# One MoE layer's dispatch inside an attention loop: TensorE's unrolled program becomes a loop of two turns, and GpSimd writes the rows that are sent out

## The chip, the cores and the metric

One NeuronCore of one Trainium2 chip. The metric is the device time of one execution in microseconds: the kernel before takes 3282.54 us, the median of 3 runs (3276.01 to 3284.56).

## What is computed

Four layers on 128 x 64 tokens of width 128 (8192 rows). Each layer adds a cross-attention with 16 heads and then a feed-forward network (FFN), both scaled by the tanh of a gate:

```python
x = x + tanh(g_xattn[l]) * xattn_l(layernorm(x), ctx, ctx)
x = x + tanh(g_ffn[l])   * ffn_l(layernorm(x))
```

Keys and values come from ctx, 64 per sequence. The FFN of layer 0 is a mixture of 8 experts with the best two taken, that of layer 1 takes the best one, that of layer 2 is a single fp8 product, and that of layer 3, whose first part the change touches, is again a mixture with two of eight experts:

```python
probs = softmax(x_flat @ router_w.T)
top_k_probs, top_k_idx = top_k(probs, 2)
cw = weights of the two, normalised by their sum
output = sum over e of cw[:, e] * (new_gelu(x_flat @ w1[e].T + b1[e]) @ w2[e].T + b2[e])
```

## The kernel before

The 8192 rows of x stay in SBUF as 64 tiles of 128 tokens. A chunk is four tiles (512 tokens), and there are CHUNKS = 16. Each attention goes through the chunks in turns: in turn u TensorE (PE) works on the attention of chunk u in four slots s = 0 to 3, one tile a slot: `scores` (L1096, psS), `p_turn` (L1105, the transposes of the softmax numerators into psT), `weigh` (L1119, weights times V into psO, and L1125, the row sums into psY). Between them lie the projections of the next chunks (`q_proj`, `k_proj`, `v_proj`), the turning of the normalised x (L1045, into psX) and the output projection of the chunk before (L1146, psX). VectorE (DVE) takes the maximum (L1541) and subtracts it (L1543), ScalarE (ACT) takes the exponential (L750) and copies the turned numerators (L756); at the end of a turn ACT inverts the row sums (L761, L763 into rden), and DVE scales the output once (L1548, one instruction per turn). GpSimd (POOL) does small steps of the layernorm (L470, L472) and adds the bias to x (L510, `x_bias`); SyncE loads ctx and spreads K into a block-diagonal kexp with 16 DMAs per turn. Attentions 0 to 2 run as loops of two turns (`Fori`) on every engine.

The last attention (layer 3) is written out on all engines (`attention_routed`), because the first half of the mixture, the dispatch, is computed inside it, some turns behind the attention:

- DVE, in turn u, takes the statistics of chunk u - 2 (`stats`, L1650 and L1653) in slot 1 and writes its normalised rows (`apply`, L1663, four TENSOR_SCALARs of 128x128) in slot 3 into a **ring** of four group buffers. A group is two chunks (8 tiles); a row has 132 elements: 128 of the token and four with its number and gates. Two buffers of the ring are in gio, one in w_ffn, one in gio3.
- PE turns the rows of chunk u - 3 from the ring (`turn_x`, L1195), multiplies by the router's weights (`route`, L1201), and in every odd turn from 5 on ranks a group's tokens within their experts by products with triangular and all-one matrices (`rank`, L1207 to L1211, into psX). The last of these products adds the counts of all groups before, kept in macc, which has two halves used in turn.
- ACT copies the logits and the ranks out of PSUM (L835 for the ranks). After a rank PE waits for that copy (semaphore rk) before it uses psX again, for L1045.
- DVE takes the routing decision of a group in 32 small steps (L1641), each of which counts up one semaphore, m_seq; steps 18 and 19 (`counts`) update macc.
- POOL does the small steps of the mixture's norm (`norm`, L560 and L562), then `x_bias`, then the **scatters**: every group is sent to the DRAM buffer xg by 16 indirect DMAs (L569) of 128 rows each, eight for the first choice in even turns from 6 on (`scatter(g, 0)`, which waits for the group's last step on DVE), eight for the second in odd turns from 7 on (`scatter(g, 1)`, without a wait). A group buffer may be rewritten when its 16 scatters have landed (semaphore sd); DVE's `apply` waits for that at the first chunk of a group from the fifth group on.

Turns run to 20 on POOL; from turn 16 on no attention is left. L1305 and L1904 stand in another stage, the first dispatch (layer 0), which also scatters rows: L1305 are products of the shared expert, L1904 reads them.

Of the kernel before, what the change touches and what calls it, by code (L numbers as in the profile page):

```python
# [61 lines left out]
def program(nc, a, out):  # L62
# [4 lines left out]
    with ExitStack() as ctx:  # L67
# [72 lines left out]
        ring.append(gio3[:, :, :])  # L140
        lgt = sb("lgt", [P, GT * E])
# [294 lines left out]
        def _(pool):  # L436
# [116 lines left out]
            def attention_routed(lay):  # L553
# [473 lines left out]
        def _(pe):  # L1027
# [159 lines left out]
            def attention_routed(lay):  # L1187
# [3 lines left out]
                def turn_x(c):  # L1191
                    e.wait_ge(m["xn"], c + 1)
                    e.wait_ge(x_up, K0 + lay * CHUNKS + c + 2 if c + 2 <= CHUNKS else K0 + (lay + 1) * CHUNKS)
# [4 lines left out]
                def route(c):  # L1198
                    e.wait_ge(m["xt_sb"], c + 1)
# [4 lines left out]
                def rank(g):  # L1204
                    e.wait_ge(m["seq"], MSTEPS[lay] * g + 18)
# [5 lines left out]
                    e.matmul(out8, ones16[:, :], macc[:, lay // 3, g % 2, :].rearrange("p (a x) -> p a x", a=1)  # L1211
# [13 lines left out]
                for u in range(CHUNKS + 4):  # L1225
                    inside = u < CHUNKS
                    c = u - 3
                    for s in range(LT):
                        if inside:
                            scores(lay, None, *ahead(u, s, 2))  # L1230
                        if s == 1 and inside:
                            q_proj(lay, None, u + 1)
                        if s == 1 and 0 <= c < CHUNKS:
                            turn_x(c)
                        if s == 2 and 0 <= c < CHUNKS:
                            route(c)
                        if s == 3 and 0 <= c < CHUNKS:
                            e.wait_ge(m["lg"], c + 1)
                        if s == 3 and u >= 5 and u % 2 == 1:
                            rank((u - 5) // 2)  # L1240
                        if inside:
                            p_turn(lay, None, *ahead(u, s, 1))
                        if s == 3 and u >= 5 and u % 2 == 1:
                            e.wait_ge(m["rk"], (u - 5) // 2 + 1)
                        if s == 3 and u + 2 <= CHUNKS:
                            ln_t(ATT[lay], None, u + 2)
                        if inside:
                            weigh(lay, None, u, s)
                        if s == 0 and inside:
                            v_proj(lay, None, u + 1)  # L1250
                        if s == 2 and inside:
                            k_proj(lay, None, u + 2)
                        if s == 3 and 0 < u <= CHUNKS:
                            out_proj(lay, None, u - 1)
                e.wait_ge(m["seq"], MSTEPS[lay] * (NG - 1) + 20)
                e.matmul(psO[:, 0:E], ones16[:, :], macc[:, lay // 3, NG % 2, :], start=True, stop=True).then_inc(m["cnt_ps"], 1)
# [12 lines left out]
            def dispatch(lay):  # L1269
# [64 lines left out]
                e.matmul(psO[:, 0:E], ones16[:, :], macc[:, lay // 3, NG % 2, :], start=True, stop=True).then_inc(m["cnt_ps"], 1)  # L1334
# [141 lines left out]
        def _(dve):  # L1476
# [143 lines left out]
            def attention_routed(lay):  # L1620
# [615 lines left out]
```

## Time and profile before

| | before |
|---|---|
| median of 3 runs | 3282.54 us (3276.01 to 3284.56) |
| the profiled execution | 3298.21 us |
| its span | 3296.4 us |
| mean granted clock of TensorE | 0.886 |
| PE, matmul / weight load | 2532.8 us (77%) / 1794.6 us (54%) |
| DVE / ACT | 1566.6 us (48%) / 1380.2 us (42%) |
| POOL | 978.3 us (30%) |
| the last attention, first to last L1548 | 2424.0 to 2828.3 us |

The rows further down are of this one profiled execution, 15.7 us above the median; its times count from the start of the span. PE stands for TensorE's matmuls and PEld for its weight loads, which run beside them. A share of the span is an average over stages of very different kinds: the attentions take turns of PE, DVE and ACT, the second halves of the mixtures are limited in other ways. "Idle before" is the time an engine stood still ahead of an instruction, with what released it; "issue" means that it waited for nothing the profile shows, and "remote" that it waited for a semaphore whose sender the profile does not name.

### The profile page before, as it was taken

What the parts mean: (1) busy time and instruction counts of PE and PEld (TensorE: products, weight loads), DVE (VectorE), ACT (ScalarE), POOL (GpSimd) and SP (SyncE); (2) the same over time, 40 slices, a digit from 0 to 9 for tenths busy, and PEclk for the clock granted to TensorE, in tenths of its full rate; (3) what the DMA queues carried; (4) which work ended last, traced back from release to release, by engine and by line L of the source; (5) the groups of instructions that cost most, each with busy time, mean ns of one, the idle gap of its engine ahead of it and who ended that gap; (6) DMA issues with size and microseconds to landing.
All of it is one profiled execution on the core that took longest, in us unless ns stands there. A gap on an engine that the chain in (4) does not pass through costs nothing. (4 is left out here: it accounts for less than half of the span.)

```text
span 3296.4 us, 74894 instructions
## 1 busy us (share of the span) xinstructions
PE 2532.8 (77%) x28202; PEld 1794.6 (54%) x28202; DVE 1566.6 (48%) x4283; ACT 1380.2 (42%) x1992; POOL 978.3 (30%) x1052
## 2 busy tenths in 40 slices
PE   4888864439997799989999969993288777358883
PEld 2555543328886455567777735551145444247773
DVE  3555544424443577622222247776667665513322
ACT  2555533213332466644545436661055444124441
POOL 4444426634444112110000000001112433634444
PEclk9999976669999899989999979996599888679997
DMA  3010101126665222100000011110011111146666
GB/s 98 22 24 20 23 16 38 39 80 195 197 192 153 78 53 61 34 3 0 0 0 0 1 44 45 41 41 11 11 32 31 37 35 37 44 144 191 189 186 219
DMA packets 143775, 219.56 MB, mean 67 GB/s; under 512 B 27177, under 2 KB 94513, under 8 KB 143026
## 3 DMA queue, kind: packets, MB, share of 16 engines
q1 hardware_dynamic: 96930, 90.25, 10.8%
q10 hardware_dynamic: 29232, 90.37, 8.8%
q0 software_dynamic: 17408, 36.21, 3.2%
q8 instruction: 128, 2.10, 0.3%
q14 instruction: 77, 0.63, 0.1%
HBM read 157.48 MB, written 43.61 MB: 61 GB/s over the span
## 5 line engine op out<-in xcount | busy, mean ns | idle before, releaser
L1541 DVE TENSOR_REDUCE mx<-psS 128x16 f32<-128x1024 f32 x264 | 322.6, 1222 | 321.9 <-PE psS L1096 294.1
L650 POOL DMA_INDIRECT yg<-ysb,yidx x288 | 279.5, 970 | 421.0 <-DVE ysb L2005 190.6
L470 POOL TENSOR_TENSOR ve<-mv,eps 128x4 f32<-128x4 f32 x102 | 20.3, 199 | 1184.4 <-DVE mv L1517 1182.3
L756 ACT ACTIVATE work<-psT 128x1024 f32<-128x1024 f32 x260 | 266.2, 1024 | 215.5 <-PE psT L1105 214.8
L750 ACT ACTIVATE work<-work 128x1024 f32<-128x1024 f32 x264 | 278.3, 1054 | 135.9 <-DVE work L1543 132.7
L1096 PE MATMUL psS<-kexp,qT 64*64 64x512 f32 x2112 | 307.6, 634 | 31.0 <-DMA kexp<-kT 15.3
L1543 DVE TENSOR_TENSOR work<-psS,mx 128x1024 f32<-128x1024 f32 x264 | 323.2, 1224 | 9.1
L1105 PEld LDWEIGHTS psT<-ident,work 128*128 128x128 f32 x2080 | 239.6, 145 | 151.5 <-issue 99.8
L1105 PE MATMUL psT<-ident,work 128*128 128x128 f32 x2080 | 288.3, 283 | 5.3 <-ACT work L756 3.3
L1381 PEld LDWEIGHTS psY<-w_ffn,work 128*128 128x128 f32 x2016 | 247.8, 192 | 9.4 <-DVE work L1976 1.2
L1381 PE MATMUL psY<-w_ffn,work 128*128 128x128 f32 x2016 | 248.5, 275 | 1.6 <-DVE ysb L1999 1.0
L1045 PE MATMUL psX<-ident,xn 128*128 128x128 f32 x408 | 78.9, 326 | 133.1 <-DVE xn L1528 103.2
L1119 PE MATMUL psO<-work,v 128*32 128x64 f32 x8192 | 172.6, 226 | 7.1 <-issue 4.4
L1125 PE MATMUL psY<-work,ones 128*32 128x128 f32 x4096 | 170.4, 279 | 5.5 <-issue 5.0
L1431 PEld LDWEIGHTS psO<-w_ffn,work 128*128 128x128 f32 x1024 | 131.3, 192 | 60.0 <-issue 49.7
L1431 PEld LDWEIGHTS psY<-w_ffn,work 128*128 128x128 f32 x1024 | 131.9, 192 | 53.5 <-issue 53.5
L1119 PEld LDWEIGHTS psO<-work,v 128*32 128x32 f32 x8192 | 130.6, 112 | 53.9 <-issue 43.4
L614 POOL DMA_INDIRECT xg<-gio,posi x128 | 125.3, 979 | 103.7 <-DVE gio L1867 64.3
L1045 PEld LDWEIGHTS psX<-ident,xn 128*128 128x128 f32 x408 | 53.5, 164 | 180.8 <-DVE xn L1528 82.3
L1528 DVE TENSOR_SCALAR xn<-x_sb,mv,rstd 128x128 f32 (+1 forms) x408 | 117.6, 352 | 66.5 <-POOL rstd L472 60.9
L1548 DVE TENSOR_TENSOR aT<-psO,rden 128x512 f32<-128x512 f32 x64 | 44.2, 691 | 196.0 <-ACT rden L763 177.2
L1431 PE MATMUL psO<-w_ffn,work 128*128 128x128 f32 x1024 | 133.2, 276 | 3.0 <-ACT work L889 2.9
(278 smaller groups left out, 4645.0 us busy)
## 6 DMA issues: line engine op xcount, KB each, us to landing
w_ffn<-in_wmoe ACTq DMA_DIRECT2D x72, 578.0 KB
w_ffn<-in_wmoe ACTq DMA_DIRECT2D x72, 576.0 KB
ctxT<-in_ctxT SPq DMA_DIRECT2D x76, 256.0 KB, 2.8
xin<-xg SPq DMA_DIRECT2D x144, 132.0 KB
kexp<-kT SPq DMA_DIRECT2D x1152, 16.0 KB
gio<-yg SPq DMA_DIRECT2D x16, 512.0 KB, 3.9
work<-yg SPq DMA_DIRECT2D x16, 512.0 KB, 6.4
yg<-ysb,yidx POOLq DMA_INDIRECT x288
```

Source lines behind the costliest of these rows:

```text
L650: e.indirect_dma_start(out=yg, out_offset=bass.IndirectOffsetOnAxis(ap=yidx[:, b, t:t + 1], axis=0), in_=ysb[:, b, t, :], in_offset=None, ...
L750: e.activation(sc[:, s % 2], sc[:, s % 2], ACT.Exp).then_inc(p_ok, 1)
L756: e.activation(pT[:, s % 2, :], psT[:, :], ACT.Copy).then_inc(pt_ok, 1)
L1045: m = e.transpose(psX[:, t * P:(t + 1) * P], xn[:, t, :], ident[:, :])
L1096: m = e.matmul(psS[64 * half:64 * half + 64, 512 * k:512 * k + 512], qT[64 * k:64 * k + 64, b, c:c + SEQ], kexp[64 * k:64 * k + 64, b, :, ...
L1105: m = e.transpose(psT[:, r * P:(r + 1) * P], sc[:, s % 2, 2 * r:2 * r + 2, :].rearrange("p a b -> p (a b)"), ident[:, :])
L1119: e.matmul(psO[32 * c:32 * c + 32, s * P + 64 * half:s * P + 64 * half + 64], v2[:, b, 2 * s + half, 64 * c + 16 * hi:64 * c + 16 * hi + 3 ...
L1125: m = e.matmul(psY[32 * c:32 * c + 32, s * P:(s + 1) * P], ones2[:, hi, :], pT[:, s % 2, at:at + P], start=(hi == 0), stop=(hi == 1))
L1381: mm = e.matmul(psY[:, t * D:(t + 1) * D], mh[:, b, k * SLOT + t * P:k * SLOT + (t + 1) * P], w[:, d0 + k * D:d0 + (k + 1) * D], start=(k ...
L1431: m = e.matmul(y[:, t * D:(t + 1) * D], hbuf[:, n % 4, t * P:(t + 1) * P], w_ffn[:, 2048 + hb * D:2048 + (hb + 1) * D], start=(hb == 0 and ...
L1541: e.tensor_reduce(mx[:, :], src, AX, ALU.max).then_inc(s_max, 1)
L1543: e.tensor_tensor(sc[:, s % 2], src, over_keys(mx[:, :]), ALU.subtract).then_inc(s_sub, 1)
```

## The change

Three things change, all in the last attention:

- PE's turns 4 to 13 become a loop of five passes of two turns (`e.Fori(0, (CHUNKS - 6) // 2)`). Turns 0 to 3 and 14 to 19 stay written out. The waits inside the loop compare with a register that the loop counts up.
- The rows that PE turns come from a new buffer of one chunk, xnf, which has the same address in every turn. DVE's `apply` writes there; it waits until the chunk before has been turned (xt_ps) and no longer for the scatters. macc has one half in use instead of two, so that its address too is the same in every turn; DVE waits for the rank product before it updates it.
- The ring is filled by GpSimd: `rows(c)` computes the same normalised rows again from x, behind `x_bias` and ahead of the scatters. It waits for the scatters that last used the buffer, and counts up the semaphore nrm, for which `scatter(g, 0)` and DVE's `stats` (with the number of two chunks before) now wait.

```diff
+        xnf = sb("xnf", [P, LT, D])
...
+                def rows(c):
+                    b = (c % 2) * LT
+                    if c >= 8 and c % 2 == 0:
+                        e.wait_ge(m[f"sd{c // 2 % 4}"], 16 * 2 * GT * (c // 8))
+                    e.wait_ge(m["rstd"], c + 1)
+                    for t in range(LT):
+                        mm = e.tensor_scalar(ring[c // 2 % 4][:, b + t, 0:D], xs(None, c, t), mmv[:, b + t, 0:1],
+                                             mrstd[:, 1, b + t:b + t + 1], ALU.subtract, ALU.mult)
+                    mm.then_inc(m["nrm"], 1)
+
                 def scatter(g, c):
                     if c == 0:
                         e.wait_ge(m["seq"], MSTEPS[lay] * (g + 1))
+                        e.wait_ge(m["nrm"], 2 * g + 2)
...
                     if u < CHUNKS:
                         x_bias(lay, None, u)
+                    if 2 <= u < CHUNKS + 2:
+                        rows(u - 2)
                     if u >= 6 and u % 2 == 0:
                         scatter((u - 6) // 2, 0)
...
-                        mm = e.transpose(psX[:, t * P:(t + 1) * P], ring[c // 2 % 4][:, c % 2 * LT + t, 0:D], ident[:, :])
+                        mm = e.transpose(psX[:, t * P:(t + 1) * P], xnf[:, t, :], ident[:, :])
...
-                    e.matmul(out8, ones16[:, :], macc[:, lay // 3, g % 2, :].rearrange("p (a x) -> p a x", a=1)
+                    e.matmul(out8, ones16[:, :], macc[:, lay // 3, 0, :].rearrange("p (a x) -> p a x", a=1)
...
-                for u in range(CHUNKS + 4):
+
+                def turn(i, u):
                     inside = u < CHUNKS
...
+                for u in range(4):
+                    turn(None, u)
+                with e.Fori(0, (CHUNKS - 6) // 2) as i:
+                    turn(i, 4)
+                    turn(i, 5)
+                for u in range(CHUNKS - 2, CHUNKS + 4):
+                    turn(None, u)
...
                 def stats(c):
...
                         e.wait_ge(m["xn"], c - 1)
+                        e.wait_ge(m["nrm"], c - 1)
...
                 def apply(c):
                     b = c % 2 * LT
-                    if c >= 8 and c % 2 == 0:
-                        e.wait_ge(m[f"sd{c // 2 % 4}"], 16 * 2 * GT * (c // 8))
+                    if c >= 1:
+                        e.wait_ge(m["xt_ps"], c)
...
-                        mm = e.tensor_scalar(ring[c // 2 % 4][:, b + t, 0:D], xs(None, c, t), mmv[:, b + t, 0:1],
+                        mm = e.tensor_scalar(xnf[:, t, :], xs(None, c, t), mmv[:, b + t, 0:1],
...
                     step(e.tensor_reduce, mcol[:, 8, :], mask16[:, :, :].rearrange("p t x -> p x t"), AX, ALU.add)
-                    step(e.tensor_tensor, macc[:, lay // 3, (g + 1) % 2, :], macc[:, lay // 3, g % 2, :], mcol[:, 8, :], ALU.add)
+                    e.wait_ge(m["rank_ps"], g + 1)
+                    step(e.tensor_tensor, macc[:, lay // 3, 0, :], macc[:, lay // 3, 0, :], mcol[:, 8, :], ALU.add)
```

The instructions of PE where its loop now begins, slots 0 and 1 of turn 4 (the line, the operation, out<-in, the shape, and how many in a row). Before:

```order
L1096 MATMUL psS<-kexp,qT 64x512 x4
L1105 MATMUL psT<-ident,work 128x128 x8
L1119 MATMUL psO<-work,v 32x64 x16
L1125 MATMUL psY<-work,ones 32x128 x8
L1064 MATMUL psQ<-w_att,ctxT 64x64 x16
L1096 MATMUL psS<-kexp,qT 64x512 x4
L1071 MATMUL psQ<-xT,w_att 128x512
L1195 MATMUL psX<-ident,gio 128x128 x4
L1105 MATMUL psT<-ident,work 128x128 x8
```

and now, with a branch into the loop and register instructions ahead of the groups whose addresses or waits the loop counts:

```order
L1277 UNCONDITIONAL_BRANCH
L1277 ISA
L1110 MATMUL psS<-kexp,qT 64x512 x4
L1115 REGISTER_ALU
L1119 MATMUL psT<-ident,work 128x128 x8
...
L1065 REGISTER_ALU
L1078 MATMUL psQ<-w_att,ctxT 64x64 x16
...
L1207 REGISTER_ALU
L1209 MATMUL psX<-ident,xnf 128x128 x4
```

The matmuls stand in the same order; the turning of the rows reads xnf instead of gio, and behind turn 5 a branch leads back to the start.

On POOL in the last attention, turn 7, an odd one, whose scatters have no wait of their own. Before:

```order
L470 TENSOR_TENSOR ve<-mv,eps 128x4
L472 TENSOR_TENSOR rstd<-ve,mhalf 128x4
L560 TENSOR_SCALAR mrstd<-mmv 128x4
L562 TENSOR_TENSOR mrstd<-mrstd,mhalf 128x4
L510 TENSOR_TENSOR x_sb<-x_sb,gbo 128x512
L569 DMA xg<-gio,posi 69632x132 x8
```

and now:

```order
L471 TENSOR_TENSOR ve<-mv,eps 128x4
L473 TENSOR_TENSOR rstd<-ve,mhalf 128x4
L561 TENSOR_SCALAR mrstd<-mmv 128x4
L563 TENSOR_TENSOR mrstd<-mrstd,mhalf 128x4
L511 TENSOR_TENSOR x_sb<-x_sb,gbo 128x512
L572 TENSOR_SCALAR w_ffn<-x_sb,mmv,mrstd 128x128 x4
L581 DMA xg<-gio,posi 69632x132 x8
```

Four instructions came in between x_bias and the eight scatters; nothing else moved on this engine.

## Rows read from the trace of the kernel before

**Rows 1.** The page's first part: engine busy us (share of the span) xinstructions.

```profile
PE 2532.8 (77%) x28202; PEld 1794.6 (54%) x28202; DVE 1566.6 (48%) x4283; ACT 1380.2 (42%) x1992; POOL 978.3 (30%) x1052
```

**Rows 2.** L1548 in attentions 1, 2, last; last from 2480 to 2525: first and last start.

```profile
L1548 DVE TENSOR_TENSOR aT<-psO,rden x14: 690/690/692, 1137.1 to 1381.7; 128x512 f32<-128x512 f32 x14
...
L1548 DVE TENSOR_TENSOR aT<-psO,rden x15: 690/692/693, 1975.9 to 2240.5; 128x512 f32<-128x512 f32 x15
...
L1548 DVE TENSOR_TENSOR aT<-psO,rden x16: 690/691/693, 2424.0 to 2828.3; 128x512 f32<-128x512 f32 x16
...
L1548 DVE TENSOR_TENSOR aT<-psO,rden x3: 691/691/693, 2482.0 to 2523.9; 128x512 f32<-128x512 f32 x3
```

**Rows 3.** Windows as long as two turns: attention 1, the last attention.

```profile
core 0: us, PE busy (x) PEld busy (x) DVE busy (x) ACT busy (x) POOL busy (x), PEclk, DMA share, GB/s
1249.30:1286.60 37.30, 35.35 (x643) 22.23 (x642) 27.91 (x46) 24.51 (x31) 7.44 (x8) 1.00 0.21 56
...
2644.30:2705.50 61.20, 46.09 (x642) 28.82 (x643) 36.77 (x100) 25.91 (x37) 23.39 (x26) 0.83 0.14 36
```

**Rows 4.** Waits in 2583 to 2644: us in total, times, longest us.

```profile
DVE aT L1548 <- ACT rden L763: 15.2, 2, 10.0
...
ACT rden L761 <- remote: 8.7, 1, 8.7
ACT rnk L835 <- remote: 7.9, 1, 7.9
```

**Rows 5.** Timeline, turn 6: start us, us, engine, line, instruction [idle before <-releaser].

```profile
2539.56 1.10 POOL L569 DMA_INDIRECT xg<-gio,posi  x1 [3.21 <-DVE gio L1641]
...
2542.41 0.17 PEld L1125 LDWEIGHTS psY<-work,ones 128*32 128x32 f32 x3 [0.58 <-issue]
...
2543.93 0.27 PE L1125 MATMUL psY<-work,ones 128*32 128x128 f32 x1 [0.39 <-issue]
...
2548.62 0.97 POOL L569 DMA_INDIRECT xg<-gio,posi  x1 [0.30 <-issue]
...
2551.90 0.60 ACT L761 ACTIVATE rden<-psY 128x512 f32<-128x512 f32 x1 [8.66 <-remote]
```

**Rows 6.** Timeline, turn 11, an odd one.

```profile
2690.18 1.10 POOL L569 DMA_INDIRECT xg<-w_ffn,posi  x1 [0.16 <-issue]
...
2694.00 0.19 PE L1211 MATMUL psX<-macc,ones 128*128 128x64 bf16 x1
...
2699.26 0.97 POOL L569 DMA_INDIRECT xg<-w_ffn,posi  x1 [0.30 <-issue]
...
2702.11 0.22 ACT L835 ACTIVATE rnk<-psX 128x64 f32<-128x64 f32 x1 [6.81 <-remote]
...
2702.38 1.12 PE L1045 MATMUL psX<-ident,xn 128*128 128x128 f32 x4 [7.29 <-ACT rnk L835]
```

**Rows 7.** DMA queues from 2536.5 to 2555: packets, MB, share of 16 engines.

```profile
q0 software_dynamic: 256, 0.54, 9.0%
q1 hardware_dynamic: 256, 0.26, 7.8%
```

**Rows 8.** DMA queues over six turns, 2583 to 2767: PE's instruction packets.

```profile
q8 instruction: 15, 0.25, 0.6%
```

**Rows 9.** Timeline of the first dispatch stage, within a burst of scatters.

```profile
588.87 2.05 PE L1305 MATMUL psY<-w_ffn,work 128*128 128x128 f32 x8 [5.50 <-DVE x_sb L1904]
...
595.59 0.75 DVE L1904 SCALAR_TENSOR_TENSOR x_sb<-psY,tg,x_sb 128x512 f32<-128x512 f32 x1 [6.87 <-issue]
```

**Rows 10.** DMA queues in the loop of attention 2, 2100 to 2200: all there are.

```profile
q1 hardware_dynamic: 3472, 3.97, 17.0%
```

**Rows 11.** Groups on POOL: busy us, mean ns of one, idle before.

```profile
L510 POOL TENSOR_TENSOR x_sb<-x_sb,gbo 128x512 f32<-128x512 f32 x6 | 7.7, 1286 | 0.0
...
L560 POOL TENSOR_SCALAR mrstd<-mmv 128x4 f32<-128x4 f32 x6 | 1.4, 238 | 0.0
```

**Rows 12.** Timeline of POOL, first scatter of turn 16.

```profile
2834.29 1.10 POOL L569 DMA_INDIRECT xg<-gio,posi  x1 [0.71 <-issue]
```

More of the change, by code:

```diff
@@ L1189, in attention_routed, with turn_x, route @@
                 m = MO[lay]
-                def turn_x(c):
-                    e.wait_ge(m["xn"], c + 1)
-                    e.wait_ge(x_up, K0 + lay * CHUNKS + c + 2 if c + 2 <= CHUNKS else K0 + (lay + 1) * CHUNKS)
+                def turn_x(i, u):
+                    e.wait_ge(m["xn"], val(i, u, 1, -2))
+                    e.wait_ge(x_up, val(i, min(u, CHUNKS + 1), 1, K0 + lay * CHUNKS - 1))
                     for t in range(LT):
-                        mm = e.transpose(psX[:, t * P:(t + 1) * P], ring[c // 2 % 4][:, c % 2 * LT + t, 0:D], ident[:, :])
+                        mm = e.transpose(psX[:, t * P:(t + 1) * P], xnf[:, t, :], ident[:, :])
                     mm.then_inc(m["xt_ps"], 1)
-                def route(c):
-                    e.wait_ge(m["xt_sb"], c + 1)
+                def route(i, u):
+                    e.wait_ge(m["xt_sb"], val(i, u, 1, -2))
                     for t in range(LT):
@@ L1202, in route, with group, rank @@
                     mm.then_inc(m["r_ps"], 1)
-                def rank(g):
-                    e.wait_ge(m["seq"], MSTEPS[lay] * g + 18)
+                def group(i, u, per, plus):
+                    return per * ((u - 5) // 2) + plus if i is None else i * per + (per * ((u - 5) // 2) + plus)
+                def rank(i, u):
+                    e.wait_ge(m["seq"], group(i, u, MSTEPS[lay], 18))
                     out8 = psX[:, GT * E:2 * GT * E].rearrange("p (t x) -> p t x", t=GT)
@@ L1224, in attention_routed @@
                 p_turn(lay, None, 0, 0)
-                for u in range(CHUNKS + 4):
+                def turn(i, u):
                     inside = u < CHUNKS
-                    c = u - 3
+                    routed = 3 <= u < CHUNKS + 3
+                    ranked = u >= 5 and u % 2 == 1
                     for s in range(LT):
                         if inside:
-                            scores(lay, None, *ahead(u, s, 2))
+                            scores(lay, i, *ahead(u, s, 2))
                         if s == 1 and inside:
[L1232 to L1240, printed above, removed]
+                            q_proj(lay, i, u + 1)
+                        if s == 1 and routed:
+                            turn_x(i, u)
+                        if s == 2 and routed:
+                            route(i, u)
+                        if s == 3 and routed:
+                            e.wait_ge(m["lg"], val(i, u, 1, -2))
+                        if s == 3 and ranked:
+                            rank(i, u)
@@ L1241, in attention_routed @@
                         if inside:
-                            p_turn(lay, None, *ahead(u, s, 1))
-                        if s == 3 and u >= 5 and u % 2 == 1:
-                            e.wait_ge(m["rk"], (u - 5) // 2 + 1)
+                            p_turn(lay, i, *ahead(u, s, 1))
+                        if s == 3 and ranked:
+                            e.wait_ge(m["rk"], group(i, u, 1, 1))
                         if s == 3 and u + 2 <= CHUNKS:
-                            ln_t(ATT[lay], None, u + 2)
+                            ln_t(ATT[lay], i, u + 2)
@@ L1247, in attention_routed @@
                         if inside:
-                            weigh(lay, None, u, s)
+                            weigh(lay, i, u, s)
                         if s == 0 and inside:
-                            v_proj(lay, None, u + 1)
+                            v_proj(lay, i, u + 1)
                         if s == 2 and inside:
-                            k_proj(lay, None, u + 2)
+                            k_proj(lay, i, u + 2)
                         if s == 3 and 0 < u <= CHUNKS:
-                            out_proj(lay, None, u - 1)
+                            out_proj(lay, i, u - 1)
@@ L1255, in attention_routed @@
+                for u in range(4):
[5 more added lines that the diff above has]
+                    turn(None, u)
                 e.wait_ge(m["seq"], MSTEPS[lay] * (NG - 1) + 20)
-                e.matmul(psO[:, 0:E], ones16[:, :], macc[:, lay // 3, NG % 2, :], start=True, stop=True).then_inc(m["cnt_ps"], 1)
+                e.matmul(psO[:, 0:E], ones16[:, :], macc[:, lay // 3, 0, :], start=True, stop=True).then_inc(m["cnt_ps"], 1)
@@ L1333, in dispatch @@
                 e.wait_ge(m["seq"], MSTEPS[lay] * NG)
-                e.matmul(psO[:, 0:E], ones16[:, :], macc[:, lay // 3, NG % 2, :], start=True, stop=True).then_inc(m["cnt_ps"], 1)
+                e.matmul(psO[:, 0:E], ones16[:, :], macc[:, lay // 3, 0, :], start=True, stop=True).then_inc(m["cnt_ps"], 1)
             def experts(lay):
```

## The prediction, before the run

> **What bounds the kernel now.** The page says TensorE (PE) is busy for 77% of the span [rows 1]; a share says nothing of one stage, so I went to the last attention and asked for the pace of its turns. L1548 runs once per turn on VectorE (DVE), so the distance between its first and last start, divided by the turns between, is the pace [rows 2]. In attention 1 it is (1381.7 - 1137.1) / 13 = 18.8 us, in attention 2 (2240.5 - 1975.9) / 14 = 18.9 us; PE runs a loop in both. In the last attention, where PE's program is written out, it is (2828.3 - 2424.0) / 15 = 27.0 us. Turns 4 and 5 of it, with routing but no scatters yet, take (2523.9 - 2482.0) / 2 = 20.9 us each (last row of the group). The busy time per stretch adds [rows 3]: two turns of attention 1 take 37.3 us, with PE busy for 35.4 of them and granted 1.00 of its clock; two turns with scatters take 61.2 us, with PE busy for 46.1 at a mean clock of 0.83. From turn 6 to turn 15, then, each turn loses about 30.6 - 20.9 = 9.7 us, some 97 us in all. The change aims at this stretch, and everything hangs on what causes the loss.
>
> The waits name it [rows 4]: ScalarE (ACT) waits 8.7 us before L761 and 7.9 us before L835, both times for semaphores of PE that the profile books as "remote". In an even turn [rows 5] the eight scatters of GpSimd (POOL) run from 2539.56 to 2549.6. From 2541.7 on PE's program, issued by whole groups before, comes a few instructions at a time with 0.6 to 1.2 us between (one such pause in the rows); the last L1125 is issued at 2543.93, and L761, which only needs that, starts at 2551.90, two microseconds after the last scatter. In an odd turn [rows 6] PE trickles nothing: the rank product L1211 is issued at 2694.00 and takes 0.19 us, but L835 sees it at 2702.11, again 1.9 us after the end of the burst (2699.26 + 0.97 = 2700.2), and PE then stands still for 7.3 us waiting for L835. So PE's signals come late as long as a burst runs.
>
> **Is it the fetching of instructions?** That is what a loop on PE would remove. Between 2536.5 and 2555.0, all 512 packets that the DMA engines move belong to the scatters and to the spread of K; none is an instruction packet [rows 7], and yet this stretch holds a full stall. Over three pairs of turns PE does fetch, 15 packets for 2 x 3 turns [rows 8], but the stall is as long without one as with one, and in the odd turn every instruction up to the wait was issued in time. The first dispatch stage, which scatters too and spreads no K, shows the same lateness: the product L1305 ends at 590.9, its reader L1904 starts at 595.59 [rows 9]. I therefore tie the loss to the burst of scatters, not to the way PE's program is stored. The bursts stay.
>
> **The change part by part.**
> - *PE's loop over turns 4 to 13.* It removes fetches that I price at nothing. A loop of this size needs none once it runs: in 100 us of attention 2 q1 alone carries packets [rows 10]. The costs are the register instructions (hidden: attention 1 with them keeps 18.65 us a turn) and the entry. 13 x 18.65 is 242.5 against the 244.6 that [rows 2] give, so the entry costs 2.1 us at most; 0 is the other bound, I take **+1.0**.
> - *What a rule says against it.* Every back edge could cost as much as the entry; [rows 2, 3] show it does not. The Trainium skill (Runtime: NRT & Kernel Launch, section Instruction fetch mechanics) says that a taken branch out of the buffered window forces a fetch and that kernels therefore prefer unrolled code. By that rule the four back edges would be paid each time; the trace does not agree, as attention 1 holds 18.65 us with a back edge every second turn.
> - *DVE's L1663 writes xnf instead of the ring.* Same four operations, same length: 0. Its wait on the scatters of four groups before goes (it is in no row of [rows 4], so nothing is won) and one on the previous turning of xnf comes, which lies two slots back in PE's order: 0. The new wait of L1650 on GpSimd's rows of two chunks before: 0 as long as POOL is not a turn behind. The new wait of macc on the rank product: behind it on DVE stands only L1548, which waits for ACT's L763, and so for PE's signals, up to 10.0 us anyway [rows 4]: 0.
> - *POOL's rows().* Four TENSOR_SCALARs of 128x128 per chunk, 16 chunks, behind x_bias and ahead of the scatters. The trace has no such row on POOL. Below: L560, 128x4, 0.24 us; above: L510, 128x512 of two inputs, 1.29 us [rows 11]. L510 less the fixed 0.24 is 2.05 ns a column; with one tensor read instead of two I halve that: 0.24 + 128 x 1.0 ns = 0.37 us, **1.5 us a chunk** (bounds 1.0 and 5.1). The Trainium skill (GPSIMD Engine Reference, section When to use GPSIMD) calls an elementwise operation of one input roughly line-rate and one of two inputs about twice as slow; halving the column part is in line with that, while at the two-input rate a chunk would cost 2.0 us and the sum 4 us more.
> - *Where those 1.5 us lie.* In an even turn the scatters wait for DVE's gates behind 3.2 us of idle POOL [rows 5]: hidden. In an odd turn the first scatter follows x_bias at once, with 0.16 us between [rows 6]: the burst starts 1.5 us later and, since PE's signals come back about 1.9 us after its end, so does the next turn. Turns 7, 9, 11, 13, 15: 5 x 1.5 = **+7.5**. Behind turn 15 only POOL's scatters are left, back to back until the barrier; rows() of chunks 14 and 15 stand ahead of them, less the 0.7 us that POOL idles there now [rows 12]: 3.0 - 0.7 = **+2.3**.
>
> Sum: 1.0 + 7.5 + 2.3 = +10.8 us. The profiled execution took 3298.21 us, 15.7 above the median of the runs (3282.54); on it the sum gives 3309.0, on the median 3293.3. About 0.3%, 9.8 us, is what a measurement of this kernel can tell from no change, so the forecast sits on that edge.
>
> **Rivals.**
> - *A, the loop cures the stall.* For: the trickle hits PE only where its program is written out, PE's idle time there is booked as issue, and no stage has both a loop on PE and scatters, so nothing refutes it directly. Against: [rows 6, 7, 9]. Turns 6 to 13 would run at 20.9 us: 4 pairs x (61.2 - 41.8) = -77.6. POOL has room: eight scatters 1.27 us apart, which [rows 6] span with 10.0 us, and some 5 us of small operations. Left of the costs: turn 15, tail, entry, 4.8. Net -72.8: **3209.7**, faster.
> - *A', only the even turns' trickle is fetching*, the odd turns' lateness is not: 4 x -9.7 = -38.8, and the costs of the forecast stay, 10.8: -28.0, **3254.5**.
> - *B, POOL is slow at these operations*, each like L510: 5.1 us a chunk. Odd turns 5 x 5.1 = 25.7, even turns 5 x (5.1 - 3.2) = 9.5, tail 9.5, entry 1: +45.7, **3328.2**. It decides from 3.2 us a chunk on, where even turns lose too.
> - *C, back edges cost like the entry*: 2.1 more for each of four and 1.1 at the entry, +9.5 on the forecast: **3302.8**.
>
> **How the numbers follow.** The forecast gets 0.56: three separate observations speak for it, but the cause of the late signals is not known. Its own range is 3284 to 3303 (below: the shifted burst costs the odd turns nothing and the entry is free, which leaves 2.3; above: 2.0 us a chunk and a full entry, 10.0 + 3.3 + 2.1 = 15.4; and some noise on both sides); half of it lies above +9.8. A gets 0.20, A' 0.14, B 0.06, C 0.04. Faster: A + A' = 0.34. Slower: half of the forecast, B and C = 0.38. Within 0.3%: 0.28. The range must reach down to A for 8 in 10, since the forecast with A' and C holds only 0.74: 3203 to 3306, with B left out.
>
> **What would show it.** If I am right, L835 and L761 still wait 7 to 9 us each for "remote", pairs of turns take 62 to 63 us, odd bursts start 1.5 us later behind x_bias, and the GpSimd row of 128x128 reads 0.3 to 0.5 us. Pairs of 42 to 45 us in the loop while turn 14 still stalls mean A; short even turns alone mean A'. A burst of scatters with no late signal would make the whole reading of the stall wrong.

## The result and the profile after

The changed kernel takes 3287.75 us, the median of 9 runs (3283.48 to 3295.73), beside 3277.81 us (3273.41 to 3285.88, 9 runs) of the kernel before on the same chip. The ratio is 1.0025, with a 95% interval of 1.0014 to 1.0036: 8 us slower by the ratio, within 0.3% (the two medians lie 9.9 us apart). The prediction said 3293.3 us, +10.8 on the kernel before. The sum came close, but two of its terms were wrong in opposite directions, and the stall under it was about three quarters smaller in every later run that scatters in the turns. Both are told below.

The profiled execution of the changed kernel took 3286.43 us, 1.3 below its median (that of before stood 20 above the median of its 9 runs). Against [rows 1], GpSimd (POOL) is busy 53 us longer and VectorE (DVE) 10 us; the page's first part:

```profile
PE 2537.8 (77%) x28202; PEld 1793.4 (55%) x28202; DVE 1576.8 (48%) x4283; ACT 1380.3 (42%) x1992; POOL 1031.0 (31%) x1116
```

The instruction that runs once per turn, now L1575, in the last attention (duration min/median/max, first and last start), answers to the third of [rows 2]:

```profile
L1575 DVE TENSOR_TENSOR aT<-psO,rden x16: 691/692/693, 2412.4 to 2817.6; 128x512 f32<-128x512 f32 x16
```

That is 405.2 us for 15 turns, and was 404.4 (404.36 and 405.20 with one more digit). Two turns in the window view, beside the last of [rows 3]:

```profile
core 0: us, PE busy (x) PEld busy (x) DVE busy (x) ACT busy (x) POOL busy (x), PEclk, DMA share, GB/s
2634.70:2696.30 61.60, 48.25 (x645) 29.03 (x641) 37.64 (x101) 25.82 (x36) 29.84 (x34) 0.83 0.13 35
```

61.6 us for two turns, and 61.2 before: the loop took nothing off. The stall is there in the loop too. The waits of two turns in the loop, 2572 to 2634 (us in total, times, longest):

```profile
POOL ve L471 <- DVE mv L1544: 26.9, 2, 13.7
DVE aT L1575 <- ACT rden L777: 19.4, 2, 10.4
ACT rden L775 <- remote: 16.5, 2, 9.1
```

Against [rows 4], the wait for the row sums now comes in both turns (L775, once L761), and the wait for the rank is no longer among those for "remote". An odd turn shows why (the rank product is now L1228, its reader L849):

```profile
2620.97 1.11 POOL L581 DMA_INDIRECT xg<-gio,posi  x1 [0.18 <-issue]
...
2621.86 0.19 PE L1228 MATMUL psX<-macc,ones 128*128 128x64 bf16 x1
...
2622.09 0.22 ACT L849 ACTIVATE rnk<-psX 128x64 f32<-128x64 f32 x1 [1.71 <-PE psX L1228]
```

The product comes 0.9 us into the burst, where it came 3.8 us into it before [rows 6], and is seen 0.04 us after its end. GpSimd's rows hold the burst back, and TensorE works on meanwhile. The timeline of one burst in the loop shows what [rows 5] showed for the written-out program:

```profile
2590.11 1.11 POOL L581 DMA_INDIRECT xg<-gio,posi  x1 [0.18 <-issue]
...
2592.37 0.15 PEld L1139 LDWEIGHTS psY<-work,ones 128*32 128x32 f32 x3 [0.61 <-issue]
...
2593.11 0.38 PE L1139 MATMUL psY<-work,ones 128*32 128x128 f32 x2 [0.32 <-issue]
...
2599.19 0.97 POOL L581 DMA_INDIRECT xg<-gio,posi  x1 [0.30 <-issue]
...
2602.34 0.60 ACT L775 ACTIVATE rden<-psY 128x512 f32<-128x512 f32 x1 [9.13 <-remote]
```

TensorE (PE) begins to trickle 2 us into the burst, its last row-sum product starts at about 2593.1, and ScalarE (ACT) sees it at 2602.34, 2.2 us after the burst's end (2599.19 + 0.97 = 2600.16). And there is nothing to fetch for PE: from 2510 to 2760 these are all the queues that carry packets, and the one that brings PE's instructions (q8, [rows 8]) is not among them:

```profile
q1 hardware_dynamic: 3392, 4.40, 7.7%
q0 software_dynamic: 2048, 4.33, 5.3%
q14 instruction: 7, 0.06, 0.1%
```

What GpSimd's rows cost stands in its groups (busy us, mean ns of one), 2572 to 2756, beside [rows 11]:

```profile
L572 POOL TENSOR_SCALAR gio<-x_sb,mmv,mrstd 128x128 f32<-128x128 f32 x24 | 19.3, 813 | 0.0
...
L511 POOL TENSOR_TENSOR x_sb<-x_sb,gbo 128x512 f32<-128x512 f32 x6 | 7.7, 1291 | 0.0
```

0.81 us each, 3.25 us a chunk, where the prediction had 0.37 and 1.5. Behind the last turn they stand ahead of the scatters (timeline of POOL, beside [rows 12]):

```profile
2822.98 3.23 POOL L572 TENSOR_SCALAR gio<-x_sb,mmv,mrstd 128x128 f32<-128x128 f32 x4 [0.18 <-POOL mrstd L563]
2826.39 1.11 POOL L581 DMA_INDIRECT xg<-gio,posi  x1 [0.18 <-issue]
...
2837.96 3.28 POOL L572 TENSOR_SCALAR gio<-x_sb,mmv,mrstd 128x128 f32<-128x128 f32 x4
```

From the last L1548 or L1575 to the start of the last scatter it is 67.8 us before and 73.8 after (67.79 and 73.85): +6.1. With +0.8 in the turns, that is 6.9 of the 8.2 us that the ratio gives. The rest lies in stages that the change does not touch, which vary by several microseconds from one execution to the next: from the last scatter to the end it is 391 to 402 us over all the traces of this study, with no order by program (b_again below, the kernel before itself, has 392.4 where the first trace has 400.3).

**About half of the loss is longer busy time of TensorE, most of it at a lower clock.** The ten turns from 6 to 15 in the window view (columns as in [rows 3]): the kernel before, the changed kernel, and, from the runs below, b_again (the kernel before once more) and e3_before_tail (no bursts in the turns):

```profile
2523.90:2828.30 304.40, 229.69 (x3190) 141.95 (x3187) 181.78 (x488) 128.31 (x179) 115.63 (x128) 0.83 0.14 36
```

```profile
2512.50:2817.60 305.10, 238.11 (x3189) 142.00 (x3187) 185.38 (x489) 128.77 (x179) 147.95 (x168) 0.84 0.13 36
```

```profile
2517.90:2751.50 233.60, 194.57 (x3190) 126.47 (x3188) 181.57 (x488) 128.67 (x179) 115.75 (x128) 0.97 0.18 48
```

```profile
2510.10:2718.70 208.60, 183.47 (x3190) 120.30 (x3188) 181.14 (x488) 127.61 (x180) 36.16 (x48) 1.00 0.12 27
```

For the same 3190 matmuls TensorE is busy 229.7, 194.6 and 183.5 us. In the first comparison the granted clock falls to its lower level, 1.2 GHz, once in each of these turns, nine times for 10.2 us. The first time in the kernel before:

```profile
2546.80:2557.00 10.20, 7.96 (x62) 4.34 (x66) 3.78 (x5) 2.73 (x5) 2.19 (x3) 0.50 0.12 31
```

There it falls 4.4 us behind a pause of the trickle (2542.4 in [rows 5]), and in the odd turns of that kernel while TensorE stands still for L835. So of the 96 us by which the first comparison's ten turns are longer than those without bursts, 46 us are longer busy time of TensorE and the rest is standing still. An estimate from the last row, half of 7.96 us in each of ten turns, puts 40 us down to the clock. No run kept the late signals and the full clock, so what each would cost by itself is open.

### The profile page after: what moved, and what is told of

It is laid out like the page before. It is cut to its first block and busy times, and to the rows that moved or that the text cites. A ratio compares the mean times of both kernels' runs of the same rounds, so it can differ in the third digit from the quotient of the medians.

```text
span 3284.6 us, 75138 instructions
## 1 busy us (share of the span) xinstructions
PE 2537.8 (77%) x28202; PEld 1793.4 (55%) x28202; DVE 1576.8 (48%) x4283; ACT 1380.3 (42%) x1992; POOL 1031.0 (31%) x1116
## 3 DMA queue, kind: packets, MB, share of 16 engines
q1 hardware_dynamic: 96930, 90.25, 10.8%
## 5 line engine op out<-in xcount | busy, mean ns | idle before, releaser
L1555 DVE TENSOR_SCALAR xn<-x_sb,mv,rstd 128x128 f32 (+1 forms) x408 | 123.8, 368 | 66.5 <-POOL rstd L473 60.8
L1575 DVE TENSOR_TENSOR aT<-psO,rden 128x512 f32<-128x512 f32 x64 | 44.3, 692 | 219.3 <-ACT rden L777 219.3
L1373 PE MATMUL psX<-ident,xin 128*128 128x128 f32 x288 | 56.2, 278 | 107.4 <-DMA xin<-xg 106.1
L1071 PE MATMUL psQ<-ctxT,w_att 128*128 128x512 f32 x180 | 110.2, 697 | 32.9 <-ACT kT L718 18.2
```

Of the source, the lines that this page charges most:

```text
L1555: m = e.tensor_scalar(xn[:, t, :], xs(i, u, t), mv[:, t, 0:1], rstd[:, t:t + 1], ALU.subtract, ALU.mult)
```

## The experiments

**Theory S**: a turn costs TensorE's own 20.9 us plus a stall that a burst of scatters causes, wherever in the turn the burst lies and however TensorE's program is stored; GpSimd's rows cost in the tail alone. Its rivals: the loop gained what GpSimd's rows then gave back (A), and the prediction's own step, that a burst which starts later makes the turn longer by as much.

The kernels below ran on three chips, those that are measured beside one figure of the kernel before on one chip with it. There it took 3212 to 3220 us, not 3278 as in the first comparison. So ratios are compared, and stages by their traces.

### The loop undone, and the rows given to VectorE

```diff
-                with e.Fori(0, (CHUNKS - 6) // 2) as i:
-                    turn(i, 4)
-                    turn(i, 5)
-                for u in range(CHUNKS - 2, CHUNKS + 4):
+                for u in range(4, CHUNKS + 4):
                     turn(None, u)
```

> The changed kernel with TensorE's turns 4 to 13 written out again; xnf, GpSimd's rows and the single macc stay. Theory S (a turn with scatters costs TensorE's own 20.9 us plus about 10 us in which the burst of eight scatters holds up its signals, however its program is stored): within 3 us of the changed kernel's 3288 us, turns from 6 on still 31 us. Rival A (the loop took away a stall and GpSimd's rows, at 3.26 us a chunk instead of the 1.5 forecast, gave it back): the unrolled one is slower than the changed kernel, by 16 us if the odd turns pay 3.26 us each.

In the next one the two waits for nrm (in `scatter` and in `stats`) go as well:

```diff
-                    if 2 <= u < CHUNKS + 2:
-                        rows(u - 2)
...
                         mm = e.tensor_scalar(xnf[:, t, :], xs(None, c, t), mmv[:, b + t, 0:1],
                                              mrstd[:, 1, b + t:b + t + 1], ALU.subtract, ALU.mult)
                     mm.then_inc(m["xn"], 1)
+                    if c >= 8 and c % 2 == 0:
+                        e.wait_ge(m[f"sd{c // 2 % 4}"], 16 * 2 * GT * (c // 8))
+                    for t in range(LT):
+                        e.tensor_scalar(ring[c // 2 % 4][:, b + t, 0:D], xs(None, c, t), mmv[:, b + t, 0:1],
+                                        mrstd[:, 1, b + t:b + t + 1], ALU.subtract, ALU.mult)
```

> The changed kernel with the ring filled by VectorE (a second set of four TENSOR_SCALARs behind apply) instead of GpSimd. Theory S: in the trace of the changed kernel the stage is 6.9 us longer than before, 6.0 of them behind the last turn, where two chunks of GpSimd's rows stand ahead of the scatters; so this version wins back about 6 us: 3281 to 3283 us, the turns unchanged at 31 us. Rival (GpSimd's rows cost in the turns, the loop hides it): more than 10 us faster than the changed kernel. Rival (VectorE's second set costs 1.4 us in each turn): slower than the changed kernel.

Measured beside 3213.72 us of before: e1_unroll 3219.51 us, ratio 1.0015 (1.0003 to 1.0027); e2_dve_rows 3212.55 us, 0.9995 (0.9983 to 1.0007). Their rows of the scaling instruction in the last attention, e1_unroll first:

```profile
L1572 DVE TENSOR_TENSOR aT<-psO,rden x16: 691/692/692, 2415.8 to 2747.6; 128x512 f32<-128x512 f32 x16
```

```profile
L1572 DVE TENSOR_TENSOR aT<-psO,rden x16: 690/692/692, 2410.4 to 2744.5; 128x512 f32<-128x512 f32 x16
```

331.8 us for the 15 turns with TensorE's program written out, 334.1 with the loop; the tails to the last scatter are 74.2 and 67.5 us. Written out, the changed kernel stands at 1.0015 of before, and with its loop at 1.0014 (a_again, below): by these intervals the loop is worth less than some 6 us either way, which speaks against A. (The turns alone can't say it more closely: further down one program differs by almost 20 us between two executions.) GpSimd's rows cost the tail 6.7 us, and the two medians lie 7.0 us apart. What no theory had: the turns take 332 us, not 404. So this tells of the loop where the stall is short; for the long one there are the rows of the first comparison, where the loop stalls with no instruction packet for TensorE.

### No bursts in the turns, with and without the loop

The ring gets eight group buffers, so that no buffer is used twice, and all 128 scatters stand behind the last turn.

```diff
-                    if u >= 6 and u % 2 == 0:
-                        scatter((u - 6) // 2, 0)
-                    if u >= 7 and u % 2 == 1:
-                        scatter((u - 7) // 2, 1)
-                scatter(NG - 1, 1)
+                e.wait_ge(m["seq"], MSTEPS[lay] * NG)
+                for g in range(NG):
+                    scatter(g, 0)
+                    scatter(g, 1)
```

> The kernel before with a ring of eight group buffers, so that all 128 scatters can stand behind the last turn; TensorE's program stays written out. Theory S: without bursts turns 6 to 15 run at about 20.9 us instead of 30.6 (-97 us), and the tail has 80 more scatters at 1.275 us (+102 us): about 3283 us, no rest of a stall in the turns. Rival A (the stall is the fetching of an unrolled program): the turns stay near 30 us, the total about 3375 us.

> The changed kernel with the same ring of eight buffers and all scatters behind the last turn: a loop on TensorE and no bursts. Theory S: the same 20.9 us a turn as e3_before_tail, the total within 5 us of it. Rival A: turns at 20.9 here but not in e3_before_tail, 90 us between the two.

Measured: 3312.57 us (1.0315 of before, 1.0296 to 1.0335) and 3311.62 us (1.0308, 1.0292 to 1.0324). The scaling instruction, e3_before_tail (written out) first, then e4_loop_tail:

```profile
L1547 DVE TENSOR_TENSOR aT<-psO,rden x16: 690/691/692, 2410.3 to 2718.7; 128x512 f32<-128x512 f32 x16
```

```profile
L1572 DVE TENSOR_TENSOR aT<-psO,rden x16: 690/692/692, 2405.1 to 2715.1; 128x512 f32<-128x512 f32 x16
```

308.4 and 310.0 us: without bursts turns 6 to 15 run at 20.86 and 20.99 us, as forecast, with a written-out program as with a loop. That is the clearest word against A: a written-out program that fetches its instructions (25 packets for TensorE in these ten turns) does not stall unless there are scatters. The total was missed by 30 us, and by far more as a difference: it was to be 5 us above the kernel before and is 99, since I had taken a saving of 97 us from the first comparison; here the bursts in the turns had cost only some 24 (332 to 334 against 308 to 310), while in the tail the 80 scatters cost 122 us (189.5 against 67.5). 102 of these are 80 x 1.275, and the other 20 are mostly the wait for the last group's decision, which in this version stands ahead of all the scatters: the first one starts 27.3 us behind the last scaling instruction, and in b_again 6.0.

### The same kernels on one chip

> The changed kernel itself once more, beside the kernel before and the three below on one chip, since the kernel before took 3278 us beside it the first time and 3214 us beside e1_unroll. Theory S: the turns are as those of e1_unroll within 3 us and the tail has the 6 us of two chunks of rows; 4 to 8 us slower than before.

> The kernel before itself, for its trace on this chip. If the length of the stall goes with the chip or the day, turns 6 to 15 have one pace in both traces of this batch that scatter in the turns, between 20.9 and 31 us.

Measured beside 3211.54 us of before: the changed kernel 3217.94 us, 1.0014 (1.0002 to 1.0026); the kernel before under this label 3214.84 us, 1.0005 (0.9989 to 1.0022), which is how far two sets of runs of one kernel can lie apart. The scaling instruction in b_again:

```profile
L1548 DVE TENSOR_TENSOR aT<-psO,rden x16: 690/690/693, 2418.0 to 2751.5; 128x512 f32<-128x512 f32 x16
```

333.5 us, and 332.9 in a_again; the tails 67.8 and 74.2. The program of b_again is that of the first trace, line for line. Of the 71 us between the two, 35 are TensorE's shorter busy time in the window rows above: its clock is at the lower level for some 14 of these 234 us, not 100 of 304. The waits show the rest. The waits of ACT in the first trace of before, from 2527 to 2783 (eight turns), and then in b_again from 2533 to 2700 (seven):

```profile
ACT rden L761 <- remote: 34.6, 4, 8.7
...
ACT rnk L835 <- remote: 30.5, 4, 7.9
```

```profile
ACT rden L761 <- remote: 8.4, 5, 2.1
...
ACT rnk L835 <- PE psX L1211: 4.6, 3, 1.5
```

An odd turn in the timeline of b_again, its burst from 2604.50 on, against [rows 6]:

```profile
2608.33 0.19 PE L1211 MATMUL psX<-macc,ones 128*128 128x64 bf16 x1
...
2608.56 0.22 ACT L835 ACTIVATE rnk<-psX 128x64 f32<-128x64 f32 x1 [1.51 <-PE psX L1211]
```

In the middle of a burst ScalarE sees the rank product 0.04 us after its end; in [rows 6] it took 7.9 us. The row sums are seen 2.3 to 3.7 us after their product in six of the ten turns of b_again, and 1.4 us after it in the other four, as in every turn without a burst; in the first trace of before it is 7.7 to 8.3 us in the even turns. The scatters do not differ: in both traces each takes 0.97 us (the first of a burst 1.1), and a burst's first packet moves 1.7 us after its start. What made the lateness so much longer in the first comparison stays open: it may go with the chip or with its state at the time. No later run showed it.

### What of a burst stalls TensorE

Both kernels are e3_before_tail with something in the place of the bursts.

```diff
+                    if u >= 6:
+                        for t in range(GT):
+                            jk[0] += 1
+                            e.tensor_tensor(junk[:, :], junk[:, :], junk[:, :], ALU.add).then_inc(m["sc_done"], 1)
+                            e.wait_ge(m["sc_done"], jk[0])
```

> e3_before_tail (ring of eight, all scatters behind the last turn) with eight GpSimd TENSOR_TENSORs of 128x512 in place of each burst: GpSimd as busy, no DMA. Theory S, scatters are what stalls TensorE: turns stay at 20.9 us. Rival (GpSimd's being busy in the turns, by its share of VectorE's data path or its late layernorm steps): turns as long as those of b_again.

```diff
+                    if u >= 6:
+                        for t in range(GT):
+                            e.dma_start(jd[(u * GT + t) * P:(u * GT + t + 1) * P, :], junk[:, :]).then_inc(m["sc_done"], 16)
```

> e3_before_tail with eight plain DMAs of 128x132 from GpSimd's queue into fixed rows of a spare DRAM tensor in place of each burst. If the transfers and their 128 pieces each stall TensorE, turns are as long as those of b_again; if it is the indirect form, whose row addresses GpSimd works out, turns stay near 20.9 us. I expect the first, since the late signals began a microsecond or two into the burst, when packets flow.

Measured, one execution each: 3383.52 and 3317.09 us. The scaling instruction and, for e5_fill, one of VectorE's groups (2550 to 2700), with the same group in e3_before_tail behind it:

```profile
L1555 DVE TENSOR_TENSOR aT<-psO,rden x16: 690/691/693, 2411.8 to 2769.1; 128x512 f32<-128x512 f32 x16
```

```profile
L1535 DVE TENSOR_SCALAR xn<-x_sb,mv,rstd 128x128 f32<-128x128 f32 x23 | 21.2, 981 | 0.0
```

```profile
L1527 DVE TENSOR_SCALAR xn<-x_sb,mv,rstd 128x128 f32<-128x128 f32 x28 | 7.7, 340 | 0.0
```

e6_direct, with the DMA issues in 2520 to 2700 (KB each, us to landing):

```profile
L1554 DVE TENSOR_TENSOR aT<-psO,rden x16: 690/692/692, 2412.6 to 2721.2; 128x512 f32<-128x512 f32 x16
```

```profile
jd<-junk POOLq DMA_DIRECT2D x72, 66.0 KB, 2.0
```

With eight plain DMAs of a scatter's size per turn the turns stay at 20.87 us: I had expected the stall here, and was wrong. They go through the same queue (q0) as 256 packets a burst, as the scatters do, and in less time, 4 to 6 us against 9.3. So neither the packets nor their landing stall TensorE. What is left is the indirect form. But two things differ beside it: GpSimd issues the eight plain DMAs in 4.3 us where eight scatters take 10, and their rows go to fixed places one behind the other. No run tells these apart from what GpSimd does within an indirect instruction, so the mechanism stays open. With GpSimd busy on tensor work for 8 x 1.05 us in a turn instead, turns take 25.75 us, which my expectation had excluded, but by another way: ScalarE never idles for the row sums there and sees every rank product 0.04 us after its end, while VectorE's TENSOR_SCALARs of L1535, most of which fall beside the filler, take 981 ns on average instead of 340. Over the ten turns VectorE is busy 228 us (181 in e3_before_tail), 23 of the 47 us in this line and the rest in the small steps of the routing decision; that is nearly the 49 us by which the turns grew. So there are two separate costs of a busy GpSimd in these turns. GpSimd's rows bring a little of the second: in the changed kernel the mean of VectorE's L1555 in the last attention is 392 ns, against 345 for L1528 in the first trace of before and 344 in b_again.

### GpSimd's rows in the turns and in the tail

```diff
+                    if c < CHUNKS - 2:
+                        for t in range(LT):
+                            e.tensor_scalar(spare[:, t, :], xs(None, c, t), mmv[:, b + t, 0:1],
+                                            mrstd[:, 1, b + t:b + t + 1], ALU.subtract, ALU.mult)
                     for t in range(LT):
                         mm = e.tensor_scalar(ring[c // 2 % 4][:, b + t, 0:D], xs(None, c, t), mmv[:, b + t, 0:1],
```

> The changed kernel with GpSimd computing the rows twice in each turn (first into a spare buffer), for all chunks but the last two, so that the tail stays as it is: 3.26 us more of GpSimd ahead of each burst. The prediction's step (a burst that starts later delays the turn by as much): 5 odd turns x 3.26 = 16 us slower than the changed kernel, or 32 if even turns pay too. Theory S (a turn is TensorE's work plus the stall, wherever in the turn the burst lies): within 3 us of the changed kernel, which stands 0.14 to 0.25% above before.

In e9_last_two GpSimd's `rows` ends with chunk 13, and VectorE fills the ring for chunks 14 and 15 behind its `apply`, as in e2_dve_rows.

```diff
-                    if 2 <= u < CHUNKS + 2:
+                    if 2 <= u < CHUNKS:
                         rows(u - 2)
```

> The changed kernel with the rows of chunks 14 and 15 alone, those behind which the tail's scatters wait, filled by VectorE. If the whole difference to the kernel before is the tail's 2 x 3.26 us of GpSimd, this is within 0.1% of before and its tail is 67 to 68 us instead of 74. If the rows of the other chunks cost as well, it stays above.

Measured beside 3220.16 us of before: e8_double 3214.45 us, 0.9984 (0.9967 to 1.0002); e9_last_two 3208.22 us, 0.9964 (0.9945 to 0.9982). The scaling instruction, e8_double first:

```profile
L1580 DVE TENSOR_TENSOR aT<-psO,rden x16: 690/692/692, 2410.9 to 2745.9; 128x512 f32<-128x512 f32 x16
```

```profile
L1575 DVE TENSOR_TENSOR aT<-psO,rden x16: 690/692/693, 2409.7 to 2729.7; 128x512 f32<-128x512 f32 x16
```

The timeline of POOL in e8_double shows the doubled rows, and that the engine still waits for work in each turn:

```profile
2591.34 0.20 POOL L472 TENSOR_TENSOR ve<-mv,eps 128x4 f32<-128x4 f32 x1 [6.23 <-DVE mv L1549]
...
2595.56 3.21 POOL L574 TENSOR_SCALAR spare<-x_sb,mmv,mrstd 128x128 f32<-128x128 f32 x4
2598.75 3.13 POOL L577 TENSOR_SCALAR gio<-x_sb,mmv,mrstd 128x128 f32<-128x128 f32 x4
2602.05 1.15 POOL L586 DMA_INDIRECT xg<-gio,posi  x1 [0.17 <-issue]
```

Twice the rows ahead of every burst give 335.0 us for the turns, where a_again has 332.9: 2 us for 14 chunks x 3.2 us, not 16 or 32, and less than the turns of one program differ by (below). The tail, which was to stay, is 77.6 us, 3.4 more than in a_again, as the last burst in the turns slides into it. Together that is 5.5 us, still a third of 16. The medians say the same more firmly: 0.9984 of before against 0.9990 for the changed kernel on the same chip (a_third), with intervals that leave no room for 16 us, 0.5%. The prediction's step falls, here where the stall is short. In e9_last_two the tail is 67.6 us, as expected, but the turns are 320.0 us, which nothing in the edit explains. So it ran again, beside the changed kernel:

> e9_last_two once more, beside the changed kernel on the same chip: it stood at 0.9964 of before with its turns at 22.0 us, 1.3 less than those of a_again, which nothing in it should cause. If that was the chip's or the execution's, it is 0.9980 to 1.0000 of before and 6.5 us, 0.2%, below the changed kernel, all in the tail. If it is real, it is at 0.9964 again and the turns read 22.0 us again.

> The changed kernel beside e9_repeat: 1.0014 to 1.0025 of before, the tail 74 us, turns 6 to 15 at 23.3 us, or at 30.5 if this chip is like the first.

Measured beside 3216.58 us of before: e9_repeat 3212.23 us, 0.9983 (0.9967 to 1.0000); the changed kernel 3214.45 us, 0.9990 (0.9974 to 1.0007). The turns of e9_repeat:

```profile
L1575 DVE TENSOR_TENSOR aT<-psO,rden x16: 690/692/693, 2407.0 to 2746.3; 128x512 f32<-128x512 f32 x16
```

339.3 us for the same program that took 320.0, and 331.7 in a_third. With bursts in them the turns of this program differ by almost 20 us between two executions on one chip; without bursts the three traces of e3_before_tail, e4_loop_tail and e6_direct lie between 308.4 and 310.0. So some of the scatter of the ratios is this spread, and 2 us between two traces mean nothing. The tails are 67.5 and 74.2 us, but the medians lie only 2.2 us apart, so most of the tail's gain is not seen in them. The clock is part of the spread: TensorE is busy 193.0 us over the ten turns of e9_last_two, at a mean clock of 0.98, and 202.9 us in e9_repeat, at 0.95. e9_last_two is below the kernel before in both comparisons, clearly in the first; against the changed kernel on the same chip (0.9983 beside 0.9990) the intervals overlap, so that it beats both is not shown.

## Why the prediction was right, and where not

- **"I therefore tie the loss to the burst of scatters, not to the way PE's program is stored."** Right, and shown by removal: a written-out program without bursts holds 20.86 us (e3_before_tail), a loop with bursts stalls as before, with no instruction packet for it. A and A' are out. It is narrower than I had it: it takes GpSimd's indirect DMAs, the transfers by themselves do nothing (e6_direct). "Some 97 us in all" for the bursts is true of the first comparison alone; in the later ones it is some 24. And I gave the mean clock of 0.83 without pricing it: late signals and pauses are only about half of those 97 us, and TensorE's longer busy time, most of it at the lower clock, is the other half. Both kernels of the first comparison have it alike, so the forecast did not suffer.
- **"I take +1.0" for the entry.** The runs do not resolve it: 331.8 us written out, 331.7 and 332.9 with the loop. C, which charged each back edge, finds no support: the turns of the first comparison grew by 0.8 us in all, and turns without bursts take 20.99 us with the loop and 20.86 without, 1.3 us over ten turns. The rule of the Trainium skill (Runtime: NRT & Kernel Launch, section Instruction fetch mechanics), by which written-out code is to be preferred, shows no difference here beyond the spread: 331.8 us one way, 331.7 and 332.9 the other.
- **"0.24 + 128 x 1.0 ns = 0.37 us."** The step was the halving of the column part for one input. Measured 0.81 us, so a chunk takes 3.25 us, 2.2 times my figure and inside its bounds (1.0 to 5.1), at the 3.2 us from which rival B was to decide. (0.81 - 0.24) / 128 is 4.5 ns a column, more than twice what L510 shows with two inputs. The row I scaled from was another operation at another width, and a scaled duration deserved a wider place in the sum than the one value. The sentence of the Trainium skill (GPSIMD Engine Reference, section When to use GPSIMD) compares GpSimd with VectorE, about twice as slow for two inputs and roughly line-rate for one, so it gave the halving no support; and it did not hold for this form with two per-partition operands, 0.81 us on GpSimd against 0.34 on VectorE.
- **"The burst starts 1.5 us later and ... so does the next turn": +7.5.** Wrong in kind. With the true duration it would have been 16; the turns grew by 0.8 us, and twice the rows added about 2 to the turns and 3.4 to the tail. The bursts do start later, as the rank product shows (0.9 us into the burst where it was 3.8), but TensorE works on while GpSimd computes, so what it does ahead of the burst it need not do behind it: a turn is its work plus the stall. For the long stall this rests on the first comparison alone, where 8.2 us (4.6 to 11.8 by the interval) less the tail's 6.1 leave no room for 16. I had read a lag (signals come 1.9 us after the end of the burst) as a chain, without following it once around the turn. B built on the same step and falls with it, though its threshold was reached.
- **"3.0 - 0.7 = +2.3" behind the last turn.** The mechanism held, the size did not: +6.1 in the first comparison, +6.4 in a_again against b_again, from the two chunks' 3.25 us each.
- **The sum.** 10.8 forecast; 0.8 + 6.1 = 6.9 found in the traces, 8.2 by the ratio. That it came out close was luck: the rows were taken too short while the turns were charged for them. Of the signs that I named, the wait for the rank (0.04 us, not 7 to 9), the pairs of turns (61.6 us, not 62 to 63) and the row of 128x128 (0.81 us, not 0.3 to 0.5) came out otherwise. And over the three comparisons of the changed kernel (1.0025, 1.0014, 0.9990) its distance from the kernel before is a few microseconds, which the third did not show at all.

## What to carry to other kernels

Before work on an idle-looking engine is charged to a loop, follow the lag once around the cycle: if the bound engine works on meanwhile, only the place where nothing else is left, here the tail, pays for it. Dispatching inside the attention is worth it where the stall is short (here 80 scatters for 24 us in the turns, against 102 in the tail) and worth next to nothing where it is long (97); a loop on TensorE changes neither. And a stall of 10 us a turn that one trace shows deserves a second chip before a change is aimed at it, and a look at the clock: here about half of it was longer busy time of TensorE, most of it at the lower clock.

## What the runs showed of the hardware

- The kernel before took 3278 us in the first comparison and 3212 to 3220 us in the later ones, on three chips. Most of the difference is in one stage, 404 against 333 us. Within a burst of indirect DMAs ScalarE saw TensorE's row sums 7.7 to 8.3 us after their product in the first trace, 2.3 to 3.7 us after it in b_again, and 1.4 us without a burst; and TensorE's clock was at its lower level for 10.2 us in nine of ten turns of the first, and for 3.4 us in four of ten turns of b_again.
- Turns with bursts of GpSimd's indirect DMAs have pauses in TensorE's issue and late signals (30.5 or 23.4 us a turn); plain DMAs of the same size from the same engine, eight in a row, do not (20.87 us a turn, against 20.86 with none).
- A TENSOR_SCALAR of 128x128 takes 0.81 us on GpSimd and 0.34 us on VectorE; and VectorE's takes 0.98 us on average when most of them run beside GpSimd's TENSOR_TENSORs.
